# Householder reduction of a 512 x 512 matrix: the product with the reflected column moves from VectorE streams to TensorE, on three bf16 parts

## The chip, the cores and the metric

The kernel runs on one core of a Trainium2 chip. The metric is the device time of one launch in microseconds, and lower is better. A core has TensorE (PE in the rows, with its weight loads as PEld), VectorE (DVE), ScalarE (ACT), GpSimd (POOL) and SyncE (SP), each with its own stream of instructions; they wait for each other by semaphores. Each engine works through its own stream in order.

## The reference, cut to what matters

The part that the change touches is the eigendecomposition of the normalised Laplacian of `adj`:

```
deg = sum(A, axis=0) + sum(A, axis=1) - diagonal(A)
L_norm = d_inv_sqrt[:, None] * (diag(deg) - A) * d_inv_sqrt[None, :]
_, U = eigh(L_norm)                      # 512 x 512
agg = einsum('mn,bnd->bmd', U.T, features)   # features: 16 x 512 x 128
out = relu(agg @ W1 + b1) @ W2 + b2
y   = einsum('nm,bmd->bnd', U, out)
```

Ahead of it stands a graph network with eight Euler steps on x (16 x 512 x 128) and a layer norm; the layer norm's result is `features`. A second layer norm ends the kernel.

## The kernel before

Four parts follow one another. A short preparation builds the 512 x 512 matrix. Then 511 Householder columns reduce it to tridiagonal form; this is a chain, since column k+1 can only be formed once column k is reflected. A divide and conquer then finds eigenvalues and vectors, and at the end the features go through the basis and back. The Euler network is cut into 551 small pieces of TensorE work, called units here (most are one fp32 matmul with 512 moving columns, or three with 128, and some are smaller); `euler()` yields after each, and they are slipped between the columns of the Householder part. The layer norm of its result, 128 pieces of ScalarE work and then 64 more, is slipped in by `takes_norm` from column 292.

The matrix lies in four tiles of 128 rows. A column k works on the tiles that still have rows below it: four tiles for the first 127 columns, three for the next 128, two for the next 128, one for the last 128. Columns with more than one tile are called wide here, those with one narrow. The vectors of the last reflections are kept as pairs in `UR` (`pairs`, `flat`), two per column, and the matrix itself is brought up to date only once in 16 columns, in the panel steps; `npend` is the number of pairs that are pending.

One wide column, in the order in which the chain runs:

- VectorE writes the new column x into `pairs` (L1676) and raises `x_ready`.
- TensorE spreads x over all partitions with transposes (L710, `row_ready`), one for each tile. It then runs one Euler unit, unread streams `keep_clock` (L684, fp32 matmuls of the identity with 256 moving columns that nothing reads; `STREAMS` sets how many), the dot products of x with all pending pairs (L723, `dots_ready`), and the product for the column before (L675).
- VectorE corrects the matrix's next column (L1488, L1497, L1509), forms the second vector of the pair before (L1516) and then, once for each tile, multiplies 512 - k - 1 columns of the matrix by the spread x and sums them (L1582): this is the product of the matrix and x.
- ScalarE takes the root of the norm (L1242) and copies five numbers (L1244, `root_ready`). GpSimd forms signs from them (L1068 to L1072) and VectorE the scalars.
- VectorE adds the correction for the pending pairs (L1488, L1497), so y is ready (L1626); two dot products (L1632, L1634, `y_ready`) are summed over partitions by TensorE (L777, `cy_ready`), and VectorE forms the next x (L1666, L1676).
- After L777 TensorE takes the row of the pending pairs at the pivot (L702) and a second Euler unit.

In columns with three or more tiles the units stand ahead of the dot products and after L777; with two tiles they stand before and after L777. In the panel steps TensorE forms the update of one tile (L770) ahead of L777, and VectorE adds it to the matrix (L1570). All of this is in program order: there is no scheduler. fp32 matmuls take two passes each, so the rows count two weight loads and two matmuls for each.

## Time and profile before

| | us |
|---|---|
| median of the runs | 3944.32 |
| lowest and highest of 3 runs | 3918.97, 3945.27 |
| span of the profiled execution | 3918.1 |
| the run that stands nearest to that span | 3918.97 |

The span runs from the first to the last instruction; the run's time is 0.9 us more. In the profile TensorE and VectorE are both busy for most of the span, at 2790.1 us and 3270.7 us. The granted clock is the share of TensorE's full 2.4 GHz that it was given: 1.0 is 2.4 GHz and 0.5 is 1.2 GHz, and a mean between them is a mixture of stretches at the two.

### The profile page before, as it was taken

The numbers are of one execution on the slowest core, as the hardware profiler recorded it, in microseconds if no ns is written. First come the engines' busy times: TensorE is split into PE (matmuls) and PEld (weight loads), VectorE is DVE, ScalarE is ACT, GpSimd is POOL, SyncE is SP. The second block draws the span as 40 slices with busy tenths as digits, with TensorE's granted clock in tenths as the row PEclk, the third lists the DMA queues.
The fourth block names the chain that finished last, engine by engine and source line by source line (L and its number), as shares of the span: only waits on it lengthen the run. The fifth ranks groups of instructions, "written<-read, shape, count | busy, mean of one in ns | idle before, by whom it ended". The sixth has DMA issues, their size and how long they took to land.

```text
span 3918.1 us, 62251 instructions
## 1 busy us (share of the span) xinstructions
PE 2790.1 (71%) x13749; PEld 2130.1 (54%) x13749; DVE 3270.7 (83%) x19331; ACT 1093.6 (28%) x4884; POOL 841.7 (21%) x4216
## 2 busy tenths in 40 slices
PE   7999999999999999889999777772123242140088
PEld 6677777777767767667677666662022221020043
DVE  6888999999889888788877777778889999989924
ACT  2333333333333344344444333321000010000013
POOL 3242222222222222233322344440000000000000
PEclk8988999999999999898888655555556566565599
DMA  2000000000000000000000000000000000000001
GB/s 64 1 1 1 1 2 1 1 2 2 1 1 2 1 1 2 1 6 1 1 1 1 1 1 1 1 1 27 1 1 0 0 1 0 0 0 0 0 0 43
DMA packets 14584, 17.39 MB, mean 4 GB/s; under 512 B 1664, under 2 KB 11008, under 8 KB 13952
## 3 DMA queue, kind: packets, MB, share of 16 engines
q1 hardware_dynamic: 14208, 13.42, 1.1%
q8 instruction: 109, 1.79, 0.2%
q14 instruction: 267, 2.19, 0.2%
HBM read 9.22 MB, written 4.19 MB: 3 GB/s over the span
## 4 chain that ended last, share of the span: by engine, by line
DVE 46%; PE 41%; issue 7%; ACT 3%; POOL 3%; DVEq 0%; DMA 0%; POOLq 0%
PE ps L684 10%; PE ps L723 7%; DVE h L2102 4%; PE ps L777 3%; PE ps L640 3%; PE ps L710 3%; PE ps L654 2%; PE ps L662 2%; PE ps L702 2%; DVE small L1613 2%; DVE ps L1597 2%; DVE small L1603 2%; DVE small L1535 2%; PE ps L980 1%; ACT UR L1280 1%
## 5 line engine op out<-in xcount | busy, mean ns | idle before, releaser
L684 PE MATMUL ps<-ident 128*128 128x256 f32 x2992 | 820.9, 414 | 0.0
L684 PEld LDWEIGHTS ps<-ident 128*128 128x128 f32 x2992 | 566.1, 203 | 67.7 <-issue 6.4
L723 PEld LDWEIGHTS ps<-UR 128*128 128x128 f32 x2552 | 378.2, 212 | 195.6 <-DVE UR L1670 93.1
L723 PE MATMUL ps<-UR 128*128 128x41 f32 (+17 forms) x2552 | 390.8, 285 | 95.1 <-ACT UR L1280 69.6
L1068 POOL TENSOR_SCALAR small<-small 128x1 f32<-128x1 f32 x511 | 117.4, 230 | 1227.3 <-ACT small L1244 1209.4
L1242 ACT ACTIVATE small<-ps 128x1 f32<-128x1 f32 x511 | 87.4, 171 | 705.7 <-PE ps L723 705.7
L1264 ACT ACTIVATE small<-lower,small 128x1 f32<-128x1 f32 x383 | 112.9, 295 | 589.3 <-DVE small L1617 589.3
L777 PEld LDWEIGHTS ps<-small,ones 128*128 128x128 f32 x766 | 122.8, 199 | 267.3 <-DVE am L1634 253.7
L702 PE MATMUL ps<-UR,ident 128*128 128x18 f32 (+2 forms) x1020 | 231.6, 309 | 44.3 <-DVE UR L1599 44.3
L1280 ACT ACTIVATE UR<-ident,UR,small 128x1 f32<-128x1 f32 x510 | 197.1, 386 | 99.6 <-POOL small L1077 99.6
L777 PE MATMUL ps<-small,ones 128*128 128x2 f32 x766 | 150.5, 266 | 103.6 <-DVE am L1634 98.1
L702 PEld LDWEIGHTS ps<-UR,ident 128*128 128x128 f32 x1020 | 186.3, 229 | 55.2 <-DVE UR L1599 55.2
L710 PEld LDWEIGHTS ps<-ident,UR 128*128 128x128 f32 x1148 | 149.3, 144 | 108.3 <-issue 51.5
L710 PE MATMUL ps<-ident,UR 128*128 128x128 f32 x1148 | 198.3, 283 | 7.0 <-DVE UR L1477 5.1
L1076 POOL TENSOR_TENSOR small<-small,erow 128x1 f32<-128x1 f32 x510 | 96.5, 189 | 471.4 <-DVE erow L1639 410.0
L1497 DVE TENSOR_REDUCE c<-am 128x4 f32<-128x56 f32 (+24 forms) x764 | 180.4, 236 | 13.1
L1666 DVE SCALAR_TENSOR_TENSOR small<-small,ps 128x1 f32<-128x1 f32 x510 | 111.9, 219 | 86.7 <-PE ps L777 47.9
L1488 DVE TENSOR_TENSOR am<-UR,ps 128x56 f32<-128x56 f32 (+24 forms) x764 | 174.8, 229 | 0.4 <-issue 0.2
L1362 ACT ACTIVATE lanes<-lanes 128x4 f32<-128x4 f32 x48 | 9.8, 205 | 580.9 <-DVE lanes L2162 580.9
L2102 DVE RECIPROCAL h<-h 128x16 f32<-128x16 f32 (+7 forms) x48 | 160.3, 3340 | 1.6
L662 PE MATMUL ps<-G,hT 128*128 128x128 f32 x1024 | 156.0, 286 | 0.0
L956 PE MATMUL ps<-ident,m 128*128 128x128 f32 x48 | 12.0, 423 | 201.3 <-DVE small L2254 201.3
(621 smaller groups left out, 7601.7 us busy)
## 6 DMA issues: line engine op xcount, KB each, us to landing
out<-xs SPq DMA_DIRECT2D x16, 256.0 KB, 2.3
m<-in_adj SPq DMA_DIRECT2D x1, 1024.0 KB, 5.4
before<-c_before SPq DMA_DIRECT2D x1, 1024.0 KB, 4.7
notafter<-c_notafter SPq DMA_DIRECT2D x1, 1024.0 KB, 8.2
sib<-c_sib SPq DMA_DIRECT2D x1, 448.0 KB, 3.0
own<-c_own SPq DMA_DIRECT2D x1, 384.0 KB, 3.3
iota<-c_iota SPq DMA_DIRECT2D x1, 256.0 KB, 2.7
h<-c_lanes SPq DMA_DIRECT2D x1, 186.0 KB, 2.4
```

Of the source, the lines that this page charges most:

```text
L640: last = nc.tensor.matmul(ps[6 + n % 2][:, :], xs[:, j, b * D:(b + 1) * D], mat[:, j, :], start=(j == 0), stop=(j == T - 1))
L662: last = nc.tensor.matmul(ps[6 + n % 2][:, tile(i)], Zt[r][i][:, tile(m)], terms[STEP3 * third + r], start=(third == 2 and r == 0), stop=( ...
L684: nc.tensor.matmul(ps[1][:, 0:2 * P].rearrange("p (a d) -> p a d", a=2), ident[:, 0:P], ident[:, 0:P].unsqueeze(1).broadcast_to([P, 2, P]) ...
L702: nc.tensor.matmul(ps[4][:, 0:2 * npend], over(one), flat[:, tp, 2 * first:2 * k], start=True, stop=True).then_inc(pivot_row_ready, 1)
L710: last = nc.tensor.transpose(ps[0][:, j * P:(j + 1) * P], over(x_of(j)), ident[:, 0:P])
L723: last = nc.tensor.matmul(ps[2][:, 0:2 * npend + 3], over(x_of(j)), flat[:, j, 2 * first:2 * k + 3], start=(j == tp), stop=(j == T - 1))
L777: nc.tensor.matmul(ps[3][:, 8:10], ones[:, :], CY, start=True, stop=True).then_inc(cy_ready, 1)
L1068: z(ts(SG, AL, 0.0, 0.5, ALU.is_ge, ALU.subtract))
L1280: nc.scalar.activation(pairs[:, tp, k, 0:1], ident[:, pp:pp + 1], ACT.Identity, scale=U1, bias=pairs[:, tp, k, 0:1]).then_inc(u_ready, 1)
L1488: return h_.mark(tt(mine.rearrange("p (t l s) -> p t l s", t=n_on, s=2), pairs[:, tiles, first:first + npend, :], swapped.unsqueeze(1).bro ...
L1497: return h_.mark(nc.vector.tensor_reduce(out[:, 0:n_on], mine.rearrange("p (t l) -> p t l", t=n_on), AX.X, ALU.add))
L2102: g(nc.vector.reciprocal(Rm, Rm))
```

## The change

The matrix is no longer kept in fp32 in `A` and `Vt`. It is kept as three bf16 parts (`parts`, `PARTS = 3`) whose sum is the fp32 value, twice, so that a panel can write the new one while the old is read; `big` holds both. x is split into three bf16 parts as well (`xsp`): the upper half of its fp32 word, the upper half of the rest, and the rest. For each pair of row tile and column tile, and each part of the matrix, TensorE loads the 128 x 128 bf16 block as weights and passes the three parts of x through: three moving columns. That makes 3 n^2 matmuls in a column with n tiles: 48, 27 and 12. ScalarE copies the sums beside VectorE's products with the pending pairs, and one VectorE sum over all of them gives y (`summed`).

The spread of x and its semaphore, the VectorE streams, the two copies that masked x (the pair is now written twice by one instruction), and the unread streams (from column 8 on) are gone. The corrected column of the matrix is formed in the column itself and no longer at the start of the next one. The panel steps change: TensorE sums the three old parts and the update in PSUM (three bf16 matmuls with the identity and one fp32 matmul for each tile), ScalarE stores the first and the second part, VectorE subtracts twice. A panel takes 5 + n columns (four where one tile is left) and not 3 + n. Wide columns with four tiles now carry one Euler unit and no longer two; so do three-tile columns in panel steps. The units end at column 374. The layer norm starts at column 390 and does two pieces in a column. The load of `own` moves behind the Householder part, since its tile holds the narrow matrices meanwhile.

```diff
-NORMS_FROM = 292
+NORMS_FROM = 390
-STREAMS = {4: (2, 3, 5), 3: (2, 2, 4), 2: (0, 0, 1), 1: (0, 0, 0)}
-BY_TENSOR = 5
+PARTS = 3
+NORMS_AT_ONCE = 2
...
+        def steps_of(n_on):
+            return 5 + n_on if n_on > 1 else 4
...
-            wanted = (1, 0, 1) if n_on > 2 else (0, 1, 1) if n_on == 2 else (0, 0, 0)
-            extra = (0, STREAMS[n_on][place], 0)
+            wanted = (0, 1, 1) if n_on == 2 or n_on == 3 and not panel else (0, 0, 1)
+            extra = (0, 0, 0)
             if k < 8:
+                wanted, extra = (0, 0, 0), (0, 2, 2)
...
+                def tile_product(m):
+                    for j in range(tp, T):
+                        for q in range(PARTS):
+                            last = nc.tensor.matmul(ps[3][:, 16 + 3 * m:19 + 3 * m], parts[current[k]][:, q, j, m * P:(m + 1) * P],
+                                                    xsp16[:, j, :, 1], start=(j == tp and q == 0),
+                                                    stop=(j == T - 1 and q == PARTS - 1))
+                    return last
...
-                if n_on > 1:
-                    for j in range(tp, T):
-                        last = nc.tensor.transpose(ps[0][:, j * P:(j + 1) * P], over(x_of(j)), ident[:, 0:P])
-                    last.then_inc(row_ready, 1)
-                for _ in range(euler_units(k)[0]):
-                    next(state, None)
-                if n_on > 1:
-                    keep_clock(halves_of[k][0])
                 for j in range(tp, T):
                     last = nc.tensor.matmul(ps[2][:, 0:2 * npend + 3], over(x_of(j)), flat[:, j, 2 * first:2 * k + 3],
                                             start=(j == tp), stop=(j == T - 1))
                 last.then_inc(dots_ready, 1)
+                if n_on > 1:
+                    if k:
+                        reflected_product(k - 1)
+                    pe.wait_ge(split_ready, k + 1)
+                    pe.wait_ge(x_copied, k + 1)
...
+                    for m in range(tp, T - 1):
+                        tile_product(m)
+                    pivot_row()
+                    tile_product(T - 1).then_inc(products_ready, 1)
...
+                            for q in range(PARTS):
+                                nc.tensor.matmul(banks[i % 3][:, cols], ident16, old[:, q, t0 + i, cols],
+                                                 start=(q == 0), stop=False)
+                            nc.tensor.matmul(banks[i % 3][:, cols], panel_rows[0][:, (t0 + i) * P:(t0 + i + 1) * P],
+                                             panel_rows[1][:, cols], start=False, stop=True).then_inc(panel_ready, 1)
...
+                        act.wait_ge(products_ready, k + 1)
+                        nc.scalar.activation(am[:, 0:n_on * width].rearrange("p (t l) -> p t l", t=n_on)[:, :, 2 * npend:width],
+                                             ps[3][:, 16 + 3 * tp:16 + 3 * T].rearrange("p (t q) -> p t q", q=3),
+                                             ACT.Copy).then_inc(product_parts_ready, 1)
...
-                    for i in range(n_on - product_by_tensor(k)):
-                        h_.post(stt(out=scratch[i][:, w], in0=mat[:, tp + i, w], scalar=1.0, in1=ps[0][:, w],
-                                    op0=ALU.mult, op1=ALU.mult, accum_out=y0[:, i:i + 1]))
...
+                has_rest = h_.mark(tt(xsp[:, on, 1], x_now, pairs16[:, on, k, 1, 1], ALU.subtract))
...
+                tt(xsp[:, on, 2], xsp[:, on, 1], xsp16[:, on, 1, 1], ALU.subtract).then_inc(split_ready, 1)
...
+                if npend:
+                    dve.wait_ge(pivot_row_ready, k)
+                    has_column = products(on, n_on, first, npend, ps[4], am[:, 216:432])
+                    h_.wait(has_products)
+                panel_rests(k)
+                dve.wait_ge(product_parts_ready, k + 1)
+                summed(y[:, here], n_on, npend, am[:, 0:216]).then_inc(y_done, 1)
```

The first place is TensorE's stream for one column with four tiles and no panel step (column 60). Before, from the pivot row of the column ahead to the second unit (L640 is a unit):

```order
501 L702 MATMUL ps<-UR,ident 128x22
502 L640 MATMUL ps<-AsT,xs 128x512
503 L710 MATMUL ps<-ident,UR 128x128 x4
504 L640 MATMUL ps<-AsT,xs 128x512
505 L723 MATMUL ps<-UR 128x27 x4
506 L675 MATMUL ps<-small,ones 128x1
507 L684 MATMUL ps<-ident 128x256 x5
508 L777 MATMUL ps<-small,ones 128x2
```

The same column in the changed kernel, where L750 is the dot products, L703 the old L675, L737 the new product, L730 the pivot row, L819 the old L777, and L617 and L628 are units:

```order
461 L617 MATMUL ps<-m,before 128x512
462 L750 MATMUL ps<-UR 128x27 x4
463 L703 MATMUL ps<-small,ones 128x1
464 L737 MATMUL ps<-cw,big 128x3 x36
465 L730 MATMUL ps<-UR,ident 128x24
466 L737 MATMUL ps<-cw,big 128x3 x12
467 L819 MATMUL ps<-small,ones 128x2
468 L628 MATMUL ps<-h,AsT 128x1 x4
```

The transposes, one unit and the five streams went; 48 matmuls with three moving columns came, 36 of them ahead of the pivot row, and the pivot row moved ahead of L819.

The second place is TensorE's stream for column 300, with two tiles. Before, when the units had already ended:

```order
2553 L702 MATMUL ps<-UR,ident 128x22
2554 L684 MATMUL ps<-ident 128x256 x2
2555 L710 MATMUL ps<-ident,UR 128x128 x2
2556 L723 MATMUL ps<-UR 128x27 x2
2557 L675 MATMUL ps<-small,ones 128x1
2558 L684 MATMUL ps<-ident 128x256 x3
2559 L777 MATMUL ps<-small,ones 128x2
```

In the changed kernel, where L682 is a unit:

```order
2428 L682 MATMUL ps<-hT,m 128x512
2429 L750 MATMUL ps<-UR 128x27 x2
2430 L703 MATMUL ps<-small,ones 128x1
2431 L737 MATMUL ps<-cw,big 128x3 x6
2432 L730 MATMUL ps<-UR,ident 128x24
2433 L737 MATMUL ps<-cw,big 128x3 x6
2434 L682 MATMUL ps<-hT,m 128x512
2435 L819 MATMUL ps<-small,ones 128x2
```

Units stand here where streams stood, and twelve matmuls of the product came in.

The third place is VectorE's stream at the start of column 60. Before:

```order
1710 L1488 TENSOR_TENSOR am<-UR,ps 128x88
1711 L1497 TENSOR_REDUCE c<-am 128x4
1712 L1509 TENSOR_TENSOR notafter<-Vt,c 128x4
1713 L1516 SCALAR_TENSOR_TENSOR UR<-notafter,small,c 128x4
1714 L1582 SCALAR_TENSOR_TENSOR junk,c<-Vt,ps 128x451
1715 L1526 SCALAR_TENSOR_TENSOR am,small<-UR 128x4
1716 L1582 SCALAR_TENSOR_TENSOR eye,c<-Vt,ps 128x451
1717 L1582 SCALAR_TENSOR_TENSOR leafsel,c<-Vt,ps 128x451
1718 L1535 TENSOR_SCALAR small<-ps,small 128x1
1719 L1540 RECIPROCAL small<-small 128x1
1720 L1582 SCALAR_TENSOR_TENSOR iota,c<-Vt,ps 128x451
1721 L1597 SCALAR_TENSOR_TENSOR ps<-small 128x1
```

In the changed kernel (L1664 and L1668 split x, L1606 is the old L1516, L1616 the old L1526):

```order
1490 L1664 TENSOR_TENSOR cw<-UR 128x4
1491 L1606 SCALAR_TENSOR_TENSOR UR<-notafter,small,c 128x4
1492 L1668 TENSOR_TENSOR cw<-cw 128x4
1493 L1616 SCALAR_TENSOR_TENSOR am,small<-UR 128x4
1494 L1629 RECIPROCAL small<-small 128x1
1495 L1624 TENSOR_SCALAR small<-ps,small 128x1
1496 L1635 SCALAR_TENSOR_TENSOR ps<-small 128x1
```

The four long streams and three of the small instructions left this place; two four-element subtractions came.

## Rows read from the trace of the kernel before

**Rows 1.** Windows view, stages and two half-clock columns: length, busy us (count), PEclk, DMA

```profile
33.00:857.00 824.00, 790.90 (x4311) 610.83 (x4310) 725.35 (x4316) 271.57 (x1226) 236.04 (x1095) 0.94 0.01 1
857.00:1547.00 690.00, 668.87 (x3830) 507.88 (x3829) 606.66 (x4119) 267.39 (x1219) 191.17 (x1024) 0.99 0.01 1
1547.00:2180.00 633.00, 567.45 (x2830) 430.00 (x2829) 512.47 (x3858) 275.22 (x1358) 191.09 (x1025) 0.89 0.01 2
2180.00:2647.00 467.00, 336.37 (x1313) 309.90 (x1311) 361.10 (x2807) 158.51 (x667) 190.26 (x1016) 0.50 0.00 1
2647.00:3918.00 1271.00, 404.88 (x1384) 251.54 (x1384) 1048.41 (x4174) 115.98 (x405) 25.02 (x26) 0.63 0.02 6
320.00:331.00 11.00, 11.00 (x43) 10.11 (x44) 5.28 (x34) 1.97 (x9) 1.49 (x8) 0.50 0.01 1
1802.00:1809.00 7.00, 7.00 (x22) 5.21 (x23) 4.52 (x31) 2.19 (x11) 1.49 (x8) 0.50 0.01 2
```

**Rows 2.** Timeline, a four-tile column at full clock (start, us, instruction, idle before)

```profile
701.00 0.57 DVE L1582 SCALAR_TENSOR_TENSOR junk<-Vt,ps 128x410 f32<-128x410 f32 x1
701.35 0.98 PE L723 MATMUL ps<-UR 128*128 128x45 f32 x8
...
702.38 1.54 PE L684 MATMUL ps<-ident 128*128 128x256 f32 x6
...
704.03 0.33 DVE L1497 TENSOR_REDUCE c<-am 128x4 f32<-128x168 f32 x1
...
704.47 0.15 DVE L1626 TENSOR_TENSOR c<-c 128x4 f32<-128x4 f32 x1
...
704.95 0.30 PEld L777 LDWEIGHTS ps<-small,ones 128*128 128x128 f32 x2 [0.81 <-DVE am L1634]
...
705.63 0.23 DVE L1676 SCALAR_TENSOR_TENSOR UR<-c,small 128x4 f32<-128x4 f32 x1
```

**Rows 3.** Timeline, a four-tile column at half clock, no panel step

```profile
319.84 0.22 DVE L1676 SCALAR_TENSOR_TENSOR UR<-c,small 128x4 f32<-128x4 f32 x1
...
322.43 1.71 PE L600 MATMUL ps<-h,m 128*128 128x3 f32 x8
...
324.00 1.88 PE L723 MATMUL ps<-UR 128*128 128x21 f32 x8
...
326.13 4.61 PE L684 MATMUL ps<-ident 128*128 128x256 f32 x10
...
328.40 0.08 DVE L1634 DVE_READ_ACCUMULATOR am<-c,UR 128x1 f32 x1
...
330.54 0.43 PE L777 MATMUL ps<-small,ones 128*128 128x2 f32 x2
...
331.25 0.23 DVE L1676 SCALAR_TENSOR_TENSOR UR<-c,small 128x4 f32<-128x4 f32 x1
```

**Rows 4.** One line, L777, around that column: ns min/median/max

```profile
L777 PE MATMUL ps<-small,ones x4: 213/283/354, 319.1 to 330.6; 128*128 128x2 f32 x4
```

**Rows 5.** Timeline, a two-tile column at half clock, with a panel step

```profile
1802.20 0.23 DVE L1676 SCALAR_TENSOR_TENSOR UR<-c,small 128x2 f32<-128x2 f32 x1
...
1809.46 0.22 DVE L1676 SCALAR_TENSOR_TENSOR UR<-c,small 128x2 f32<-128x2 f32 x1
```

**Rows 6.** Timeline, bf16 matmuls of the divide and conquer, half clock

```profile
3089.18 0.34 PEld L885 LDWEIGHTS ps<-h,split 128*128 128x128 bf16 x4 [9.40 <-DVE small L1936]
...
3089.59 2.66 PE L893 MATMUL ps<-h,split 128*128 128x128 bf16 x23
```

**Rows 7.** Timeline, narrow columns at half clock

```profile
2501.07 0.48 ACT L1141 ACTIVATE xs<-h,hT 128x128 f32<-128x128 f32 x1
...
2503.85 0.29 ACT L1261 ACTIVATE c<-c,small 128x1 f32<-128x1 f32 x1 [1.69 <-DVE small L1651]
...
2504.47 0.22 DVE L1670 SCALAR_TENSOR_TENSOR UR<-c,small 128x2 f32<-128x2 f32 x1
```

**Rows 8.** The page, one DMA issue: out<-in, engine, KB, us to landing

```profile
own<-c_own SPq DMA_DIRECT2D x1, 384.0 KB, 3.3
```

563 lines of the change are left out of this document (320 added, 243 removed).

## The prediction, made before the changed kernel ran

> **What bounds the kernel now.** I read the windows view first, cut at the stages of the Householder part. It takes 824, 690, 633 and 467 us for the columns with four, three, two and one tile, and the rest 1271 us [rows 1]. With 126, 128, 128 and 128 columns that is 6.54, 5.39, 4.95 and 3.65 us for a column. The change works on the first three stages, 2147 of the 3918 us. In them VectorE is busy for 725, 607 and 512 us and TensorE for 791, 669 and 567 us, at a granted clock of 0.94, 0.99 and 0.89 [rows 1]. So both are nearly full, and the timeline has to say who is waited for.
>
> At full clock it is VectorE in a four-tile column: its four streams take 0.57 us each, while TensorE fills itself with unread streams, six passes in 1.54 us here [rows 2]. These do not lie on the path. At half clock it is TensorE. The column from 320 us took 11.4 us (331.25 less 319.84), with TensorE busy for every one of the 11 us; y's dot product was there at 328.48 and L777 came 2.1 us later, at 330.54, behind ten passes of L684 [rows 1, 3]. The two-tile column at 1802 us took 7.3 us where the stage's mean is 4.95, again with TensorE full [rows 1, 5]. The reader should take from this that one kernel has two regimes, and that the clock chooses between them.
>
> **What the clock does.** The windows show what TensorE did at each level. In the first three stages, with units and unread streams of hundreds of moving columns, it was mostly 1.0 (2.4 GHz). In the narrow stage it stood at 0.50 (1.2 GHz), although the rows count TensorE busy for 336 of 467 us; there it ran only matmuls with few moving columns [rows 1]. The change takes the transposes, the unread streams and one of two units out of a four-tile column and puts in 48 matmuls with three moving columns each. That is work of the narrow stage's kind. I take it that one unit in a column does not hold the full clock, and that stages one to three run at half clock most of the time. This choice decides the sign.
>
> The Trainium skill, "TensorE: Matmul & The Clock Gate", section "Why this matters for your kernels", asks that TensorE be kept busy without long pauses, and says that it then keeps its full clock. By it a column packed with 48 back-to-back matmuls would be fast, which is the first rival below. The narrow stage [rows 1] speaks against reading busy that way.
>
> **The change, part by part, at half clock.** Prices first.
> - A pass of an fp32 matmul with few columns is 0.22 us: eight took 1.88 us, of which the last one's tail is 0.35, so 1.53/7 [rows 3, 4].
> - 256 fp32 columns are 0.43 us: ten passes took 4.61 us, 0.35 of it tail [rows 3]. So a unit with 512 columns (two passes) is 1.7 us and one with three times 128 is 1.3 us. With the smaller ones I take 1.45 us, an estimate from these two.
> - A product matmul: no row shows bf16 weights with three columns. The bound below is the full-clock floor, for which I take 0.03 us; that is an estimate, half of what follows. The nearest row is the second pass of L777, whose weights are ready: two passes end 0.43 us after the start and one alone takes 0.354, so 0.075 us for one more [rows 3, 4]. Four bf16 weight loads fit in 0.34 us, so loads don't hinder that [rows 6]. The bound above is the bf16 matmul with 128 columns, (2.66 - 0.31)/22 = 0.107 us [rows 6]. I take 0.075 us, since its columns are as few.
> - From the last product matmul to L777's successor TensorE has nothing of the chain to do: tail 0.28, ScalarE's copy 0.2, VectorE's sum 0.33, then 0.33 from y (704.62) to the weight load at 704.95, one added wait 0.1 and the handovers 0.15 [rows 2]. Together 1.4 us.
>
> The four-tile column then is TensorE's own sum, since each step waits for the one before: dot products 8 passes, L675's 2, the pivot row's 2, L777's 2, so 14 x 0.22 = 3.1; products 48 x 0.075 = 3.6; the 1.4 above; one unit behind L777, 1.45, which runs past the point where the next x is ready. Sum 9.5 us, against 6.54 now. 126 columns give 1200 us. A panel step puts 3 x 0.43 + 2 x 0.85 = 3.0 us ahead of L777 in four columns of each of seven panels; 1.4 of it lies in the gap, so 28 x 1.6 = 45. Stage one: 1245 us, now 824.
>
> Check of this price list on a column that the trace has: the one at 320 us by the same prices is transposes 0.9, two units of eight small passes 3.4 (1.71 each), dot products 1.7, L675 0.4, ten stream passes 4.3, L777 and pivot row 0.9, so 11.6 us; it took 11.4 [rows 3].
>
> Three tiles: 12 x 0.22 = 2.6, 27 x 0.075 = 2.0, 1.4, 1.45: 7.5 us. Where a second unit stands ahead of L777 it fills the gap, so it is 7.5 us too. 128 columns 960, with 24 panel steps of 0.8 beyond the gap 980; now 690.
>
> Two tiles: dot products 0.9; then the pivot row waits for VectorE's correction, 1.4 after L675 starts (its two passes and four or five small dependent instructions of 0.2); pivot row 0.4, six products 0.45, unit 1.45, L777 0.4, unit 1.45: 6.5 us. 120 columns with units 780 and eight without at 5.9, 47: 827; now 633.
>
> Sum of the three: 3052 against 2147, so +905. Against this stands some full clock. In the columns with two units around L777, and in the panel steps, TensorE moves hundreds of columns nearly without a pause, and the trace returned to 1.0 after such stretches. I give stages two and three a quarter of their time at full clock, where a column is 5.0 and 4.6 us (below): -80 and -60, and the panels of stage one -30. That leaves +735.
>
> **Edits beside it.** Before column 0 ScalarE makes twelve copies of 128 x 512 and VectorE subtracts in between; at about 0.6 us each some 7 us, and ScalarE's first column waits for them: +8. VectorE loses four streams and gains two sums of 200 elements and two panel subtractions for each tile; at half clock it waits for TensorE anyway. ScalarE gains panel copies that hide behind TensorE likewise, but would not at full clock in panel columns, some tenths of a us each. The layer norm's two pieces in a narrow column are 0.48 us each [rows 7]; one stands behind the root, where ScalarE sits idle for 1.69 us before L1261, so it costs nothing. If that cover were gone it would be 96 x 0.48 = 46 us. `own` now loads behind the last column, 3.3 us to landing [rows 8], beneath VectorE's sums of the diagonal; nothing to 3 us. Nothing else in the narrow stage or behind it changes.
>
> Total: 3918.97 + 735 + 8 = 4662, say 4660 us. The profiled execution's own time is the lowest of the three runs, 0.6% under the median 3944.32; I leave the forecast as the sum gives it. Its own range: with 0.03 us for a product matmul -270, -155 and -30, so 4200; with 0.107 us +190, +110 and +30, so 4990; the quarter of full clock moves it by 170 more at most, either way.
>
> **Rivals.**
> 1. The clock holds at full (faster). Then a four-tile column is: second vector of the pair 0.4 after x, dot products 8 x 0.1 = 0.8 [rows 2], L675 0.2, 36 products at half of 0.075 1.35, pivot row 0.2, 12 products 0.45, gap 1.4, and 0.91 from L777's load to the end of x (705.86 less 704.95) [rows 2]: 5.7 us, or -106 us in the stage. Three tiles: 0.4, 0.6, 1.15 until the correction, 0.2, 0.35, 1.4, 0.9: 5.0 us, -50. Two tiles 4.6 us, -40. With +8 the sum is -188: 3730 us. For it: TensorE gets 48 matmuls without a pause, and at full clock VectorE's four streams of 0.57 us are really on the path. Against it: the narrow stage's 0.50. It decides where stage one's clock stays above some 0.9. Chance 0.22.
> 2. The clock holds, and a product matmul costs 0.06 us and not 0.0375. That adds 0.0225 x 48 x 126 = 136 us in stage one and some 50 in the others, which eats the gain: 3915 us. Chance 0.06.
> 3. The forecast's case, half clock, chance 0.72.
>
> **How the numbers follow.** The forecast is case 3, 4660 us. The range takes in all of case 1's sum at its low end, 3730, and ends at 4950 above: what is left out are the dearest product matmul together with no return of the clock, and a gain beyond case 1. About 1% is what a measurement of this kernel can tell from no change. Faster by over 1% is case 1, 0.22; within 1% most of case 2, 0.05; slower 0.73. The forecast's own range is 4200 to 4990.
>
> **What would show it.** In the changed kernel's windows at the same stages: a granted clock of 0.5 to 0.6 in the four-tile stage and up to 0.7 in the two after it; four-tile columns of 9 to 10 us from x to x; TensorE without a pause but for the gap of 1.4 us, and the L819 group no longer waiting behind streams. VectorE's busy time in the first stage should fall by some 250 us, with its idle time ended by ScalarE's product copy. L737's pitch should be 0.07 to 0.08 us. The narrow stage should stay at 467 us and the rest at 1271. The prediction is wrong if matmuls with three columns hold the clock (then 1.0 in stage one and columns under 6 us), or if their pitch is outside 0.03 to 0.107 us.

## The result, and the profile of the changed kernel

The changed kernel takes 4475.23 us (median of 4 runs, 4463.9 to 4477.8); the kernel before, run beside it, 3931.64 us (3917.99 to 3945.27). The ratio is 1.137, with a 95% interval of 1.132 to 1.142: slower by 544 us. The forecast was 4660 us with a range of 3730 to 4950.

The windows view of the changed kernel, cut at its own stages (the same columns as [rows 1]):

```profile
33.00:1015.00 982.00, 864.94 (x8440) 681.58 (x8439) 513.44 (x3335) 351.42 (x1632) 236.59 (x1095) 0.51 0.01 2
1015.00:1904.00 889.00, 802.39 (x5906) 617.60 (x5905) 485.48 (x3376) 348.88 (x1636) 193.43 (x1024) 0.53 0.01 1
1904.00:2731.00 827.00, 718.34 (x3814) 528.21 (x3813) 454.40 (x3361) 342.40 (x1635) 193.89 (x1025) 0.55 0.01 2
2731.00:3201.00 470.00, 338.81 (x1310) 310.48 (x1310) 361.38 (x2804) 187.16 (x848) 191.67 (x1017) 0.50 0.00 1
3201.00:4475.00 1274.00, 411.26 (x1384) 254.54 (x1384) 1049.28 (x4174) 116.21 (x405) 25.32 (x26) 0.62 0.02 6
```

Against [rows 1] the three wide stages took 982, 889 and 827 us in place of 824, 690 and 633: +551 us, of the 557 us by which the two profiled spans differ. The narrow stage and the rest stayed within 3 us each, at 470 and 1274 us. The granted clock fell from 0.94, 0.99 and 0.89 to 0.51, 0.53 and 0.55. VectorE has 212 us less to do in stage one (513.44 against 725.35) and none of it is seen in the time. TensorE's busy time rose by 74 us in that stage, with less moved through it, at half the clock.

One four-tile column of the changed kernel at half clock, from the timeline (the column runs from the end of one L1722 to the end of the next, 504.01 to 511.23, 7.22 us; the view starts inside the unit L628, which began at 503.35):

```profile
503.56 1.63 PE L628 MATMUL ps<-h,AsT 128*128 128x1 f32 x7
503.78 0.23 DVE L1722 SCALAR_TENSOR_TENSOR UR<-cw,small 128x8 f32<-128x8 f32 x1
...
505.06 1.89 PE L750 MATMUL ps<-UR 128*128 128x31 f32 x8
...
506.76 0.56 PE L703 MATMUL ps<-small,ones 128*128 128x1 f32 x2
...
507.19 1.10 PE L737 MATMUL ps<-cw,big 128*128 128x3 bf16 x36
...
508.15 0.61 PE L730 MATMUL ps<-UR,ident 128*128 128x28 f32 x2
...
508.58 0.48 PE L737 MATMUL ps<-cw,big 128*128 128x3 bf16 x12
...
510.12 0.58 PE L819 MATMUL ps<-small,ones 128*128 128x2 f32 x2 [1.06 <-DVE am L1700]
...
510.56 0.99 PE L628 MATMUL ps<-h,AsT 128*128 128x1 f32 x4
...
511.00 0.23 DVE L1722 SCALAR_TENSOR_TENSOR UR<-cw,small 128x8 f32<-128x8 f32 x1
```

Read it as a chain. x is there at 504.01, but the Euler unit L628 still runs and the dot products start at 505.06. They take 1.89 us where [rows 2] had 0.98 at full clock. The new product takes 1.10 + 0.48 us for 48 matmuls, which is little. The pivot row L730 starts at 508.15 behind its first 36 matmuls; VectorE's L1637, for which it waits as well, had ended only at 508.05. So the 36 matmuls run beside a chain on VectorE that is nearly as long. Between the product's end and L819 lies a real pause of 1.06 us, for ScalarE's copy and VectorE's sum. The kernel before needed 11.4 us for its half-clock column, 4.61 of it in unread streams [rows 3]; so this four-tile column is not dearer in the changed kernel at the same clock (e3 below compares them without the streams). What differs is the clock, at which nearly all of them run.

The panel steps, in the same view around the column that ends at 543.03, where L806 and L808 are the three old parts and the update:

```profile
538.19 0.49 PE L737 MATMUL ps<-cw,big 128*128 128x3 bf16 x12
...
538.54 1.44 PE L806 MATMUL ps<-big,own 128*128 128x512 bf16 x3
539.91 2.07 PE L808 MATMUL ps<-qrow,junk_a 32*128 32x512 f32 x2
541.91 0.59 PE L819 MATMUL ps<-small,ones 128*128 128x2 f32 x2
```

Here L819 starts 3.72 us behind the start of the last twelve product matmuls; in the column above it was 1.54. The page's groups of the two lines that the argument is about (busy us, mean ns of one, idle before):

```profile
L1629 DVE RECIPROCAL small<-small 128x1 f32<-128x1 f32 x511 | 83.9, 164 | 796.4 <-ACT small L1329 792.1
L737 PEld LDWEIGHTS ps<-cw,big 128*128 128x128 bf16 x11088 | 497.5, 116 | 4.0 <-DVE cw L1668 4.0
...
L737 PE MATMUL ps<-cw,big 128*128 128x3 bf16 x11088 | 410.5, 167 | 3.9 <-ACT cw L1318 3.9
```

Over all 511 columns VectorE idles for 796 us ahead of the reciprocal L1629, which waits for the root that ScalarE draws out of the dot products: VectorE now waits for TensorE's dot products.

### The profile page after: what moved, and what is told of

It reads as the page before. It is cut to its first block, busy times and chain, and to the rows that moved or that the text cites. A ratio compares the mean times of both kernels' runs of the same rounds, so it can differ in the third digit from the quotient of the medians.

```text
span 4475.0 us, 77279 instructions
## 1 busy us (share of the span) xinstructions
PE 3153.3 (70%) x20965; PEld 2408.9 (54%) x20965; DVE 2883.8 (64%) x17114; ACT 1358.5 (30%) x6182; POOL 849.3 (19%) x4218
## 4 chain that ended last, share of the span: by engine, by line
PE 54%; DVE 35%; issue 5%; ACT 4%; POOL 2%; DVEq 0%; DMA 0%; POOLq 0%
PE ps L750 11%; PE ps L690 6%; PE ps L668 5%; PE ps L682 5%; PE ps L730 5%; PE ps L737 4%; PE ps L819 4%; DVE h L2216 4%; PE ps L808 3%; DVE ps L1635 2%; DVE small L1624 2%; PE ps L806 2%; PE ps L703 1%; PE ps L617 1%; PE ps L1021 1%
## 5 line engine op out<-in xcount | busy, mean ns | idle before, releaser
L750 PEld LDWEIGHTS ps<-UR 128*128 128x128 f32 x2552 | 594.1, 317 | 348.5 <-DVE UR L1722 157.0
L750 PE MATMUL ps<-UR 128*128 128x41 f32 (+19 forms) x2552 | 577.3, 375 | 115.7 <-ACT UR L1371 70.3
L1629 DVE RECIPROCAL small<-small 128x1 f32<-128x1 f32 x511 | 83.9, 164 | 796.4 <-ACT small L1329 792.1
L737 PEld LDWEIGHTS ps<-cw,big 128*128 128x128 bf16 x11088 | 497.5, 116 | 4.0 <-DVE cw L1668 4.0
L730 PE MATMUL ps<-UR,ident 128*128 128x18 f32 (+2 forms) x1020 | 310.6, 395 | 164.3 <-DVE UR L1637 164.3
L737 PE MATMUL ps<-cw,big 128*128 128x3 bf16 x11088 | 410.5, 167 | 3.9 <-ACT cw L1318 3.9
L819 PEld LDWEIGHTS ps<-small,ones 128*128 128x128 f32 x766 | 200.1, 310 | 374.6 <-DVE am L1700 264.4
L730 PEld LDWEIGHTS ps<-UR,ident 128*128 128x128 f32 x1020 | 248.1, 302 | 197.3 <-DVE UR L1637 197.3
L819 PE MATMUL ps<-small,ones 128*128 128x2 f32 x766 | 201.6, 333 | 161.8 <-DVE am L1700 161.5
L1329 ACT ACTIVATE small<-ps 128x1 f32<-128x1 f32 x511 | 87.5, 171 | 640.6 <-PE ps L750 640.2
L690 PE MATMUL ps<-G,hT 128*128 128x128 f32 x1024 | 272.6, 432 | 0.0
L690 PEld LDWEIGHTS ps<-G,hT 128*128 128x128 f32 x1024 | 231.7, 319 | 15.4 <-issue 15.4
L1577 DVE TENSOR_TENSOR am<-UR,ps 128x104 f32<-128x104 f32 (+25 forms) x764 | 188.0, 246 | 57.4 <-PE ps L730 48.2
L703 PE MATMUL ps<-small,ones 128*128 128x1 f32 x766 | 207.7, 340 | 0.9 <-DVE am L1616 0.9
L703 PEld LDWEIGHTS ps<-small,ones 128*128 128x128 f32 x766 | 198.9, 317 | 1.0 <-DVE am L1616 1.0
L1361 ACT ACTIVATE cw<-c,small 128x4 f32<-128x4 f32 (+2 forms) x382 | 113.6, 297 | 178.9 <-DVE c L1583 178.9
```

The costliest lines, as they stand in the source:

```text
L690: last = nc.tensor.matmul(ps[6 + n % 2][:, tile(i)], Zt[r][i][:, tile(m)], terms[STEP3 * third + r], start=(third == 2 and r == 0), stop=( ...
L703: nc.tensor.matmul(ps[4][:, 64:65], ones[:, :], SPART, start=True, stop=True).then_inc(s_ready, 1)
L730: nc.tensor.matmul(ps[4][:, 0:2 * npend], over(one), flat[:, tp, 2 * first:2 * k], start=True, stop=True).then_inc(pivot_row_ready, 1)
L737: last = nc.tensor.matmul(ps[3][:, 16 + 3 * m:19 + 3 * m], parts[current[k]][:, q, j, m * P:(m + 1) * P], xsp16[:, j, :, 1], start=(j == t ...
L750: last = nc.tensor.matmul(ps[2][:, 0:2 * npend + 3], over(x_of(j)), flat[:, j, 2 * first:2 * k + 3], start=(j == tp), stop=(j == T - 1))
L819: nc.tensor.matmul(ps[3][:, 8:10], ones[:, :], CY, start=True, stop=True).then_inc(cy_ready, 1)
```

## The experiments

Two questions. Is the lost clock the whole price? And what lost it: the missing streams, or matmuls with three moving columns? The kernel before took 3918.02 to 3923.91 us (medians) beside these runs.

**e1_streams_back.** The changed kernel with unread streams again, in the columns without a panel step and the first two steps of a panel. It also takes more Euler units in the late panel steps, two more with four tiles.

```diff
-            wanted = (0, 1, 1) if n_on == 2 or n_on == 3 and not panel else (0, 0, 1)
...
+            if n_on == 4:
+                wanted = (0, 2, 1) if step > 5 else (0, 0, 1)
+                if step < 2:
+                    extra = (0, 3, 1)
...
+            elif n_on == 2:
+                wanted = (0, 2, 1) if step > 3 else (0, 1, 1)
+                if step < 2:
+                    extra = (0, 1, 1)
```

> The changed kernel with fillers for TensorE put back into the wide columns: three to four unread streams of 256 columns in the gap behind the product and one or two behind the last matmul, and in the late panel steps two Euler units in the gap. The product by bf16 parts stays as it is. Theory (the clock is what made the change slow): granted clock over 0.9 in the three wide stages, columns of about 5.7, 5.2 and 4.8 us, total about 3775 us, 700 under the changed kernel and under the kernel before as well. Rival (the product on TensorE and its longer chain are slow by themselves): the streams only add work, total 4475 us or more, clock whatever it is.

Measured: 4293.59 us, ratio 1.093 (1.085 to 1.100). Windows of its stages one to three:

```profile
34.00:995.00 961.00, 947.05 (x9211) 746.99 (x9210) 501.84 (x3338) 355.63 (x1640) 239.21 (x1095) 0.68 0.01 2
995.00:1849.00 854.00, 793.86 (x6505) 584.66 (x6504) 473.75 (x3377) 348.51 (x1656) 196.53 (x1024) 0.78 0.01 2
1849.00:2570.00 721.00, 626.01 (x4270) 482.74 (x4269) 443.22 (x3360) 316.19 (x1608) 196.43 (x1024) 0.86 0.01 2
```

Neither theory as put. The streams brought the clock back in part (0.68, 0.78, 0.86), and the time fell with it, most in stage three. Four-tile columns that were at full clock from end to end (21 of them) took 5.74 us in the median, against 6.2 before. Those at half clock (42, many of them panel steps) took 9.4. The panel steps among them are no dearer than in the changed kernel (9.4 for 9.4), but plain columns are, 8.0 us for 7.2 (k62), and so are the late steps with two more units, 9.4 for 8.2 (k54, k55): at half clock the added work stands in the way. One of those at full clock, for the product's pitch (the time from the start of one matmul to the next):

```profile
343.48 1.05 PE L756 MATMUL ps<-cw,big 128*128 128x3 bf16 x36
344.44 0.40 PE L749 MATMUL ps<-UR,ident 128*128 128x18 f32 x2
344.69 0.44 PE L756 MATMUL ps<-cw,big 128*128 128x3 bf16 x12
344.99 1.54 PE L731 MATMUL ps<-ident 128*128 128x256 f32 x6
```

36 matmuls in 1.05 us, of which the last one lasts 0.165: 0.025 us from one to the next. At half clock it is (1.10 - 0.166)/35 = 0.027. The product does not care for the clock.

**e2_one_part.** The changed kernel, with the product formed from the first part of the matrix only.

```diff
-                        for q in range(PARTS):
+                        for q in range(1):
```

> The changed kernel with the product taken from the first bf16 part of the matrix alone (the other two parts of the matrix are left out of the product): 16, 9 and 4 matmuls in place of 48, 27 and 12. Theory (TensorE at half clock is the bound, a product matmul is only 0.027 us of it): 32 x 0.027 = 0.86 us less in a four-tile column, 0.49 in a three-tile one, 0.1 with two, so 109 + 62 + 13 = 185 us less: 4290 us, clock still about 0.5. Rival (the number of product matmuls explains the loss of 543 us): two thirds of it go, about 4110 us.

Measured: 4410.0 us, 65 us below the changed kernel; stages 959, 867 and 806 us at 0.51, 0.54 and 0.57. The gain is smaller than either expectation had it (185 and 365 us). Leaving out two thirds of the 11,088 product matmuls gains 65 us together. The product on TensorE is hardly the price. The theory took every spared matmul for 0.027 us of the path, and that was wrong. The column k62 took 6.97 us for 7.22, and in it the pivot row waits for VectorE:

```profile
496.86 0.63 PE L730 MATMUL ps<-UR,ident 128*128 128x28 f32 x2 [0.45 <-DVE UR L1637]
```

So of the matmuls ahead of the pivot row nearly none count, and of those behind it 8, 6 and 4 are spared in a column with four, three and two tiles: 0.027 x (8 x 126 + 6 x 128 + 4 x 128) = 62 us, which is what was measured.

**e3_before_no_streams.** The kernel before, without its unread streams.

```diff
-STREAMS = {4: (2, 3, 5), 3: (2, 2, 4), 2: (0, 0, 1), 1: (0, 0, 0)}
+STREAMS = {4: (0, 0, 0), 3: (0, 0, 0), 2: (0, 0, 0), 1: (0, 0, 0)}
...
-                units, extra = (0, left, 0), (2 * wanted[0], 2 * wanted[1] + extra[1] - 2 * left, 2 * wanted[2])
-                extra = tuple(max(0, e) for e in extra)
+                units, extra = (0, left, 0), (0, 0, 0)
```

> The kernel before with every unread stream taken out and nothing else changed. Theory (those streams held the clock, and the change lost it with them): granted clock falls to 0.5 to 0.6 in the wide stages, TensorE becomes the bound there, columns of about 7.5, 7.0 and 6.5 us, total about 4450 us, so that this edit alone costs what the whole change costs. Rival (the streams do little, the clock is held by the units and transposes): 3930 us, clock over 0.85.

Measured: 4451.68 us, ratio 1.133. Windows of its first three stages:

```profile
33.00:1086.00 1053.00, 811.21 (x3297) 628.55 (x3296) 741.45 (x4314) 278.25 (x1225) 236.05 (x1095) 0.65 0.00 1
1086.00:2006.00 920.00, 707.08 (x2967) 538.75 (x2966) 616.68 (x4117) 270.24 (x1218) 190.90 (x1022) 0.69 0.00 1
2006.00:2707.00 701.00, 494.51 (x1846) 380.29 (x1846) 526.46 (x3858) 274.83 (x1360) 193.11 (x1027) 0.52 0.01 2
```

The total came within 2 us of the theory's, but its parts did not: columns took 8.4, 7.2 and 5.5 us in the mean where 7.5, 7.0 and 6.5 were expected, at 0.65 and 0.69 in stages one and two and not at 0.5 to 0.6. So that closeness is luck. What stands is the total: with nothing of the change but its missing streams, the kernel before loses 530 us, and the changed kernel lost 544. Work that nobody reads was worth 530 us here. Stage by stage the two kernels without streams are not alike. In stages one and two this one is slower than the changed kernel (1053 and 920 us for 982 and 889) although its clock is higher. In stage three it takes 701 us at 0.52, the changed one 827 at 0.55. Two-tile columns are dearer in the changed kernel at the same clock; the next run shows how much of that is Euler units.

**e4_two_units.** The changed kernel with two Euler units in every wide column until they are used up.

```diff
-            wanted = (0, 1, 1) if n_on == 2 or n_on == 3 and not panel else (0, 0, 1)
+            wanted = (0, 1, 1) if n_on > 1 else (0, 0, 1)
```

> The changed kernel with one Euler unit ahead of L819 and one behind it in every wide column from column 8, as two-tile columns have, and no streams. Theory (half clock; the second unit lies in the gap of 1.4 us): four-tile columns stay at 7.8 us and the clock near 0.5, the units end near column 283 and the two-tile columns behind that fall from 6.5 to 5.5 us, total about 4380 us. Rival (two units are enough for the clock, as they nearly were before): clock over 0.8 in the first stage, columns under 6.3 us there, total under 4150 us.

Measured: 4447.07 us; stages 992, 940 and 741 us at 0.59, 0.54 and 0.53. A second unit does not hold the clock (0.59 in stage one for 0.51). It moves work from stage three to stages one and two: +61 and -86 us. The two-tile columns from k285 to k373, which have no unit here and two in the changed kernel, took 5.65 us in the mean against 6.61 there. So nearly 1 us of such a column is units, and without them it is close to the 5.34 us of the same columns in e3. The expected 4380 us was 67 too low; the rival, that the clock returns, is out.

**e5_wide_moving.** The same number of product matmuls in the same order, each with 60 moving columns in place of 3 (x's three, repeated by the access pattern).

```diff
-                            last = nc.tensor.matmul(ps[3][:, 16 + 3 * m:19 + 3 * m], parts[current[k]][:, q, j, m * P:(m + 1) * P],
-                                                    xsp16[:, j, :, 1], start=(j == tp and q == 0),
+                            last = nc.tensor.matmul(ps[3][:, 64 + 60 * m:64 + 60 * (m + 1)].rearrange("p (r c) -> p r c", c=3),
+                                                    parts[current[k]][:, q, j, m * P:(m + 1) * P],
+                                                    xsp16[:, j, :, 1].unsqueeze(1).broadcast_to([P, 20, 3]), start=(j == tp and q == 0),
```

> The changed kernel, but each of the 48 product matmuls of a wide column moves 60 columns (the three of x, repeated 20 times by the access pattern) in place of 3; no other work is added, and ScalarE reads three columns of each 60. Theory (the half clock is what the change costs, and the engine falls back because its product matmuls, though back to back, stream almost nothing): the clock of the stages rises above the 0.51 to 0.55 of the changed kernel, but the gaps between the matmuls stay, so it holds only in part: 0.6 to 0.8 in stage one, and the time 4150 to 4500 us (a pair 0.05 us at half clock, +1.1 us for a column at half clock, against 2 us less for a column at full clock). Rival (the clock asks only whether the engine has something to do): clock stays 0.51 to 0.55, each wide column pays 48 x 0.02 to 0.03 us more, 4475 + 382 x 1.0 = about 4850 us at most.

Measured: 4426.39 us, 49 us below the changed kernel, although the product got dearer. The windows of stages one to three, and below them the product in a four-tile column at half clock:

```profile
33.00:1091.00 1058.00, 938.76 (x8414) 770.10 (x8442) 512.95 (x3339) 354.94 (x1637) 237.00 (x1095) 0.56 0.01 2
1091.00:1899.00 808.00, 745.08 (x5909) 575.70 (x5907) 478.37 (x3379) 339.70 (x1636) 195.09 (x1024) 0.68 0.01 2
1899.00:2687.00 788.00, 687.74 (x3808) 500.72 (x3808) 450.56 (x3359) 337.90 (x1635) 194.68 (x1024) 0.63 0.01 2
```

```profile
552.41 1.96 PE L737 MATMUL ps<-cw,big 128*128 128x60 bf16 x36
554.19 0.61 PE L730 MATMUL ps<-UR,ident 128*128 128x28 f32 x2
554.62 0.78 PE L737 MATMUL ps<-cw,big 128*128 128x60 bf16 x12
```

The theory's mechanism held in stages two and three: 0.68 and 0.63 where the changed kernel had 0.53 and 0.55, with no instruction added. In stage one the clock rose only to 0.56, under the 0.6 expected, and the dearer product ((1.96 - 0.235)/35 = 0.049 us from one to the next) made the stage 76 us longer. The rival, no effect on the clock at all, is out.

**e6_wide_moving_streams.** e5 with the streams of e1; the diff is those two together.

> The kernel of e5_wide_moving with the unread streams of e1_streams_back as well. Theory: nothing of a wide column is now without streaming work on TensorE, the granted clock of the stages is above 0.95 up to k381, a four-tile column takes 5.6 us, a three-tile column 5.1, a two-tile column 4.75 (33 + 126 x 5.6 + 128 x 5.1 + 128 x 4.75 = 2000 at k382, then 467 + 1271): about 3740 us, faster than both kernels. Rival (the product of the change is itself long on TensorE, whatever the clock): full clock, but columns of 6.5 us and more, 4200 us or above. Third possibility: the clock still falls in four-tile columns as in e1_streams_back, and the time is about 4300 us.

Measured: 4002.65 us, ratio 1.023 (1.017 to 1.029). Windows of stages one to three:

```profile
35.00:884.00 849.00, 823.31 (x9182) 687.18 (x9211) 505.60 (x3337) 356.91 (x1639) 238.85 (x1095) 0.90 0.01 2
884.00:1608.00 724.00, 689.44 (x6506) 526.51 (x6505) 471.16 (x3379) 343.14 (x1656) 196.76 (x1026) 0.98 0.01 2
1608.00:2266.00 658.00, 574.05 (x4270) 440.67 (x4269) 441.14 (x3360) 311.18 (x1608) 195.48 (x1024) 0.98 0.01 2
```

This is the main result. Both means together hold the clock at 0.90, 0.98 and 0.98, and the kernel is 473 us below the changed one and 81 above the one before. It is not the 3740 us that the theory gave, and neither the 4200 of the rival. Columns at full clock from end to end took 6.18, 5.56 and 5.04 us in the mean. 126, 128 and 128 of them would be 779 + 712 + 645 = 2136 us, against 2147 in the kernel before. But those 2147 us contain the half-clock spells of the kernel before. Its own columns at full clock from end to end (some 110, 122 and 101) took 6.21, 5.32 and 4.58 us in the mean, which would be 2050 us (an estimate, as is the 2136: the columns that fell to half clock, many of them panel steps, are missing from both means). With the clock held everywhere in both, the changed design would be some 85 us behind, and all of that in the columns with three and two tiles. By this estimate the 81 us by which e6 is slower are not its spells, since the kernel before loses about as much by its own (some 97 us, and e6 some 95). Part of it may be Euler units, which e6 carries further into stage three; no run takes that apart. The plain four-tile column is shorter than before (5.76 us, where most of the plain ones took 6.1 to 6.3); here is one, from 761.37 to 767.13:

```profile
761.46 0.60 PE L731 MATMUL ps<-ident 128*128 128x256 f32 x2
761.89 0.97 PE L770 MATMUL ps<-UR 128*128 128x25 f32 x8
...
762.70 0.36 PE L719 MATMUL ps<-small,ones 128*128 128x1 f32 x2
...
762.92 1.53 PE L756 MATMUL ps<-cw,big 128*128 128x60 bf16 x36
...
764.29 0.37 PE L749 MATMUL ps<-UR,ident 128*128 128x22 f32 x2
...
764.50 0.61 PE L756 MATMUL ps<-cw,big 128*128 128x60 bf16 x12
...
764.96 1.53 PE L731 MATMUL ps<-ident 128*128 128x256 f32 x6
...
766.33 0.28 PE L839 MATMUL ps<-small,ones 128*128 128x2 f32 x2
766.47 1.10 PE L698 MATMUL ps<-h,m 128*128 128x512 f32 x2
```

But a panel has nine steps with four tiles where the kernel before had seven, and they took 6.2 to 7.1 us at full clock (k112 to k119), where the kernel before stayed at 5.6 to 6.3. What is gained in plain four-tile columns is given back there.

**e7_wide_moving_few.** e6 with fewer streams: `extra = (0, 2, 0)` in four-tile columns, `(0, 1, 0)` in the others.

> The kernel of e6_wide_moving_streams with fewer unread streams (two behind the load in four-tile columns, one in the narrower ones). Theory: if the product matmuls with 60 moving columns hold the clock nearly alone, the time is that of e6_wide_moving_streams or up to 60 us less (fewer streams in the path of the pivot), about 3700 to 3740 us; if the streams are what holds it, the clock falls below 0.8 in stage one and the time is above 4000 us.

Measured: 4044.77 us, ratio 1.034; stages 845, 728 and 687 us at 0.88, 0.96 and 0.91. The time is that of the second theory (above 4000 us), but not its clock, which stayed above 0.8. Columns at full clock are a little shorter (6.09, 5.46, 4.99 us), and what is gained so is lost again by more columns at half clock, above all in stage three.

**e8_units_in_panel.** e6 with a unit more in panel steps 2 to 5 of four-tile columns, `(0, 1, 1)` for `(0, 0, 1)`, and one stream for two in the narrower columns.

> The kernel of e6_wide_moving_streams, with one Euler unit more behind the product in panel steps 2 to 5 of the four-tile columns (where it has no stream, and where the clock fell at k19 to k24 and k50 to k58, 9 to 10.5 us a column), and one stream in place of two in three- and two-tile columns. Theory (at full clock the changed column is worth 5.7 to 6.3 us, and what is left of the 4003 us above 3922 is in the spells at half clock): the spells go, stage one takes 770 to 800 us instead of 849 us, and the time is 3900 to 3960 us, level with the kernel before. Rival (the spells do not come from the lack of work in those steps): stage one stays at 840 us or more, and the time is 4000 us or more.

Measured: 4016.03 us; stages 849, 713 and 668 us at 0.94, 0.97 and 0.95. The clock of stage one rose from 0.90 to 0.94, the spells got shorter but did not go (k50 to k55 still 8.3 to 12.2 us), and the steps with the unit cost 0.7 to 0.9 us more at full clock. The stage came out at the same 849 us, as the rival had it. Its reason, that the lack of work has nothing to do with the spells, is not borne out, since the clock rose: the cure costs what it saves.

**e9_wider_in_panel.** e6 with 108 moving columns in panel steps 1 to 8.

```diff
+        def moved(k):
+            return 108 if k % PANEL in (1, 2, 3, 4, 5, 6, 7, 8) else 60
```

> The kernel of e6_wide_moving_streams, with 108 moving columns in place of 60 in the product matmuls of panel steps 1 to 8. Theory: the same spells go by this means too; a pair of a load and a matmul takes 0.05 to 0.06 us at full clock instead of 0.038, so that these columns cost 0.6 to 0.9 us more (some 40 us over stage one), against 60 to 80 us saved: 3960 to 4000 us. Rival: spells stay, and the time is 4040 us or more.

Measured: 4072.14 us; stages 891, 743 and 658 us at 0.95, 0.98 and 0.99. The spells stayed, though less deep (k19 to k24 at 0.67 to 1.0, k50 to k57 at 0.54 to 1.0), as the rival had it. The clock is nearly whole in all three stages, and the kernel is still 154 us behind the one before. The columns of steps 1 to 8 took 7.4 to 8.4 us at full clock, about 1.2 us more than in e6, where 0.6 to 0.9 was expected. The clock is not for free: what is moved to hold it stands in the chain, unless the engine would wait there anyway.

**e10_unit_moved.** The changed kernel, with the unit of a four-tile column (and of a three-tile column in a panel step) ahead of L819.

```diff
-            wanted = (0, 1, 1) if n_on == 2 or n_on == 3 and not panel else (0, 0, 1)
+            wanted = (0, 1, 1) if n_on == 2 or n_on == 3 and not panel else (0, 1, 0) if n_on > 2 else (0, 0, 1)
```

> The changed kernel with one edit: the Euler unit of a four-tile column (and of a three-tile column in a panel step) stands behind the product, ahead of the column that waits for y, and not behind that one. At half clock the unit of 1.4 us keeps the next column's dot products from starting (their weights are in at 0.41 us, the matmuls start at 1.19 us), while the engine waits about 1.1 us for y. Theory (TensorE's own row of work sets the period at half clock, the place of a unit only decides who waits): 0.3 to 0.5 us less for each of about 126 columns, stage one 920 to 945 us in place of 982, the time 4415 to 4440 us. Rival (the load for y is then late, and the same amount is lost there): stage one 975 to 1000 us, the time 4470 us or more.

Measured: 4505.72 us, 30 us more than the changed kernel; stages 992, 915 and 816 us. The theory fell, the rival held. The same column (k62) as shown of the changed kernel, from the end of L1722 at 509.47:

```profile
509.91 1.89 PE L750 MATMUL ps<-UR 128*128 128x31 f32 x8 [0.96 <-DVE UR L1606]
511.61 0.56 PE L703 MATMUL ps<-small,ones 128*128 128x1 f32 x2
...
513.42 0.48 PE L737 MATMUL ps<-cw,big 128*128 128x3 bf16 x12
...
513.76 1.85 PE L628 MATMUL ps<-h,AsT 128*128 128x1 f32 x8
515.47 0.57 PE L819 MATMUL ps<-small,ones 128*128 128x2 f32 x2
...
516.32 0.23 DVE L1722 SCALAR_TENSOR_TENSOR UR<-cw,small 128x8 f32<-128x8 f32 x1
```

The dot products start 0.44 us behind x and no longer 1.05, but L819 starts at 6.00 us and not at 6.11: the unit of 1.85 us does not fit into the pause of 1.06. The column took 7.08 us for 7.22. In panel steps the unit and the panel's matmuls stand in a row ahead of L819, and the column took 10.5 us for 9.4; that made the sum a loss.

**e11_one_part_full_clock.** e6 with the product from the first part only, the edit of e2.

> The kernel of e6_wide_moving_streams, but the product is formed from the first bf16 part of the matrix only (16, 9 and 4 matmuls in place of 48, 27 and 12), so that the product is a coarse one and two thirds of its work on TensorE are left out. Question: at full clock the changed column takes 5.75 to 5.95 us where the one before took 6.2 in the mean; is it the product that keeps it from being shorter? Theory (it is one term of several: the pivot row's product starts only at 2.9 us after x and the last tile's matmuls stand behind it, so only 8 of the 32 spared matmuls of 0.038 us end on the path): 5.4 us for a four-tile column at full clock, 0.3 to 0.4 less, and nothing in two-tile columns. Rival (all of it is on the path): 1.2 us less, 4.6 us. The clock may fall where work is left out, so columns at full clock are what counts; if it holds, 3930 to 3970 us.

Measured: 4046.4 us, at 0.85, 0.88 and 0.92 in the wide stages. Plain four-tile columns at full clock took 5.23 us for 5.76 (k105 to k107). So 0.53 us of the 1.2 spared on TensorE were on the path, more than the theory's 0.3 to 0.4 and less than half of the rival's.

```profile
730.48 0.61 PE L756 MATMUL ps<-cw,big 128*128 128x60 bf16 x12
731.45 0.40 PE L749 MATMUL ps<-UR,ident 128*128 128x22 f32 x2 [0.35 <-DVE UR L1657]
731.69 0.31 PE L756 MATMUL ps<-cw,big 128*128 128x60 bf16 x4
```

The first twelve matmuls now end 0.35 us before the pivot row, which waits for VectorE's L1657; only what stands behind it counts in full. Still the kernel as a whole is 44 us slower than e6, and not 30 to 70 faster: with less to move, the clock fell.

**e12_mixed_streams.** e6 with one stream less behind L839: `extra = (0, 3, 0)` with four tiles, `(0, 1, 0)` with three.

> The kernel of e6_wide_moving_streams with one stream less in a four-tile column and in a three-tile column (none behind the column that waits for y). Theory (the design is level with the kernel before, not ahead of it, once the clock is held): 3960 to 4010 us, stage one 830 to 850 us, stage two 710 to 725 us, stage three 655 to 670 us. Rival (the streams behind that column were what the next column's dot products waited for): 3920 us or less, level with the kernel before.

Measured: 4035.17 us; stages 849, 738 and 662 us at 0.89, 0.94 and 0.96. Stages one and three as the theory had them, stage two 13 us over it, since the clock fell there; the sum is over the expected 4010 and far from the rival's 3920. Of the five versions with wide moving columns and streams that form the whole product (e6 to e9 and e12), e6 has the lowest median (the runs of e8, 4002.69 to 4049.08 us, overlap its 3993.71 to 4012.08), and none beats the kernel before.

## Why the prediction was right, and where it was off

The sign and its cause were right. The forecast rested on one choice, that 48 matmuls with three moving columns do not hold the clock. It was 0.51 in stage one for a forecast of 0.5 to 0.6, and 0.53 and 0.55 in stages two and three for "up to 0.7". e3 shows that losing the streams costs the kernel before as much as the whole change costs (530 and 544 us), and e6 shows it from the other side: with the clock at 0.90 to 0.98, 473 us come back. So the two designs are about level without anything that holds the clock (4452 and 4475 us) and 81 us apart with it (3922 and 4003 us). The clock is the price, and the product on TensorE gains nothing at either level.

The forecast was 185 us too high: 233 in stage one (1215 forecast) and 11 in stage two, against 60 too low in stage three. Its terms, one by one:

- **The product matmul was mis-sized.** 0.075 us was taken; it is 0.027 at half clock. That is even under the stated bound of 0.03, which was an estimate (the prediction calls it half of 0.075, which would be 0.0375). 48 x 0.048 = 2.3 us in a four-tile column, 290 us in the stage, and 27 x 0.048 x 128 = 166 us in stage two. The nearest row [rows 4] was an fp32 matmul, and its second pass of 0.075 us said nothing of a bf16 matmul with three columns. e2 adds a second finding: at 0.027 the matmuls ahead of the pivot row are hidden beside VectorE's chain to L1637, while the prediction's sum put all of TensorE's work in one row.
- **The panel steps were priced at half.** Steps with two matmul groups take 9.4 us for 7.2, and the other steps are longer too: about 13 us over one panel (0.75 + 3 x 2.2 + 3.2 + 2 x 1.0 + 0.4 at k65 to k72), 91 us over seven, where 45 stood. The work itself was close (1.44 + 2.07 us less an overlap, so 3.4, for 3.0).
- **The gap** was 1.06 us and not 1.4 (L737's end to L819's start): 43 us too much in stage one. The dot products and L703 were right, 2.13 us for ten passes of 0.22.
- **The unit was priced too low.** It took 1.71 us in the column shown (503.35 to the dot products at 505.06), and 1.64 in the mean of the 121 four-tile columns at half clock (from L819's two passes to the next dot products), where 1.45 stood: 24 us in the stage. The row of units in [rows 3] had 1.71.
- By these, stage one comes to 1245 - 290 - 43 + 24 + 46 = 982 us (the 1245 without any full clock), and it took 982; that it meets to the microsecond is chance, since the terms are rounded. The list of what stands in TensorE's row was right, and one price in it was far off.
- **The recovery was too generous.** A quarter of stages two and three at full clock was assumed, 170 us less in all. By the mean clock it was 6 and 10% of the time, and 2 to 3% in stage one. This error went the other way and hid part of the first. That stage two was forecast at 900 and took 889 is luck: the product alone was 166 us too dear, and most of what made up for it was the smaller recovery (6% for 25, so some 60 us of the 80), a pivot row that waits 0.29 us for L1637 in each column (37 us), and the unit ahead of L819, which puts 1.71 us (median) between the product's end and L819 where 1.4 stood (40 us). Stage three was forecast at 767 and took 827, of which the same share (10% for 25) explains 36; the two-tile column, 6.5 us in the list, took 6.46 in the mean of the stage.
- **The edits beside it** came to nothing visible in the sum: x of column 1 was complete at 32.7 us (33.0 before). The copies did hold column 0 up, its product started only at 28.62, but the sixteen passes of unread streams that column 0 had before (5.66 us) were gone. The narrow stage was at 470 us for 467, and the load of `own` landed in 3.1 us beneath other work.
- **What would show it**: right for the clock and the last two stages; wrong for four-tile columns of 9 to 10 us (7.2) and for L737's pitch. VectorE's busy time fell by 212 us (250 forecast), but its idle time is ended mostly by ScalarE's root L1329 and not by the product copy.

**The first rival** (full clock, 3730 us) had its columns nearly right: 5.7, 5.0 and 4.6 us were forecast, and plain columns at full clock took 5.76 in e6 (5.67 in e7), 5.0 in e5's stage two and 4.7 to 4.9 in stage three. Its sum would not have come true all the same. Of its gain of 196 us in the three stages, about 97 would have been the half-clock spells of the kernel before, since it subtracts from means that contain them (2147 us; 2050 at full clock, see e6). It left out the panel steps at full clock (6.2 to 7.1 us), and what holds the clock has a price of its own in the column: e6 to e9 and e12 are at 4003 to 4072 us. The second rival's price of 0.06 us for the pair is refuted (0.025 at full clock), although its time, about level with before, is where e6 ends for other reasons.

The rule cited from the Trainium skill, "TensorE: Matmul & The Clock Gate", section "Why this matters for your kernels", asks for a TensorE that is kept busy. In stage one the rows have it busy for 864.94 of 982 us, at 0.51, and its longest pause in the column shown is 1.06 us. To be busy in the sense of the rows did not keep the full clock here; the measurement decides against reading the rule so.

**What stays open.** Why the clock falls in some spells and not in others that look alike: e6 fell at k19 to k24, k50 to k58 and k101 to k102, and held from k103 to the end of the stage with the same instructions. The kernel before has such spells too (k35 to k41). How the loss from 0.94 to 0.51 in stage one divides among what the change took out is open too: without its streams the kernel before still has 0.65 (e3), and no run takes out the transposes alone. And whether the spells and the dearer panel steps could be removed without a new cost was not shown: the attempts (e7, e8, e9, e12) paid as much as they saved or more.

## What to carry to other kernels

Before work is moved onto TensorE, or unread work is taken off it, ask what the granted clock rests on, and take the streams out of the kernel before as a first experiment: here setting them to nothing cost 530 us, as much as the whole change. Compare two designs at the same clock, column against column, before a mean that mixes both clocks is called a gain. Count work at both clocks: fp32 passes of tens of columns take twice as long at half clock, small bf16 matmuls do not (0.027 and 0.025 us). Ask of each piece whether it stands alone on the path: two thirds of the product matmuls gave 65 us. A design that is shorter in the plain column may pay for it in the columns with extra steps; compare means over a stage, not the best column.

## What the runs showed of the hardware that was not expected

- A bf16 weight load of 128 x 128 with a matmul of three moving columns follows the last one in 0.025 us at the full clock and 0.027 us at half. With 60 columns it is 0.038 us ((1.53 - 0.199)/35, e6) and 0.049 us (e5). The Trainium skill, "TensorE: Matmul & The Clock Gate", section "Wait — 56ns, not 53.3ns?", gives a floor of about 25 ns from start to start however few the columns; by the rows here the trace agrees, and shows that the spacing hardly moves with the clock.
- The two fp32 passes of a dot product with 25 to 31 columns cost 0.97 us for eight at full clock and 1.89 at half.
- TensorE busy for 88% of a stage (864.94 of 982 us) was granted half clock almost throughout; with 60 for 3 moving columns in the same instructions the clock of stage two rose from 0.53 to 0.68.
